# Cross attention of a two-layer decoder: all eight query projections ahead of the scores, in two PSUM banks in turn, with a new table of turns

## The chip, the cores and the metric

One core of one Trainium2 chip. The metric is the time on the device of one execution, in microseconds; less is better. The kernel before took 611.25 us, the median of three runs (607.7 to 611.59 us).

## The reference, cut to what matters

The decoder has two layers. Each is a self attention, a cross attention to a context, and a feed-forward part, with a layer norm ahead of each and the result added to x. The change touches the cross attention of the first layer (16 heads of 64, model width 128, four batches of 256 tokens, a context of 256 tokens, a mask that is False everywhere here):

```python
x = x + _L0_attn_ref(...)                          # stage l0a, relative position bias
q = layernorm(x) @ Wq                              # 128 -> 1024, 16 heads of 64
k = ctx @ Wk
v = ctx @ Wv
s = q @ k.T * 64**-0.5                             # per head, causal and padding mask
x = x + (softmax(s) @ v) @ Wo + bo                 # stage l0x
x = x + bit_linear / depthwise conv feed-forward   # stage ffn
...                                                # layer 1: stages l1a, l1x, moe
```

## The kernel before, in words

The four batches are split into two lanes, A and B, of two batches (512 tokens) each. Both lanes run the same six stages (l0a, l0x, ffn, l1a, l1x, moe) on the same core; each lane has its own four PSUM banks (`bank[0]` to `bank[3]`, printed as A_banks and B_banks) and its own part of SBUF. Lane A runs ahead of lane B by about one stage, so that a stage of A stands beside another stage of B.

For each engine each lane has a program that yields between its steps, and `merged` (line 2423) takes steps of the programs in the turns that the table `TURNS` (line 2389) gives for that engine: "A4 W1 A5" is four steps of lane A, one of the weight preparation, five of lane A. Each engine carries out its merged list strictly in that order: an instruction that waits for a semaphore holds up all that stand behind it. The numbers that the programs yield (`PAIRS`, `STEP`) order steps inside a lane, where two programs of it are interleaved (`interleaved`, line 113).

The stage l0x is `cross_attention` (line 718). Its TensorE program:

- `context` (line 940): 16 jobs, eight that project the values (L951) and eight that project the keys (L953), each one matmul of 128x512 in float32, in banks 0 to 2 in turn, copied out by ScalarE (L826).
- `queries(c)` (line 956), for c = 0 to 7: one matmul of 128x512 (L966), copied out by VectorE with the scale (L868). Query 0, 2 to 7 use bank 2, query 1 uses bank 3 (`q_bank`, line 781).
- `scores(p)` (line 976), for 16 pairs of heads p (8 for each of the lane's two batches): L984 and L986, in banks 0 and 1. VectorE adds the mask and takes the largest of each row (L914), ScalarE takes the exponential with the sums (L835), VectorE inverts the sums (L932), GpSimd multiplies (L818).
- `transposed(u)` (line 989), two for each pair: three transposes (L998) into bank 2, copied out by ScalarE (L852).
- `weighted_values(g)` (line 1001): probabilities times values (L1011) in bank 3, copied out by VectorE (L928) into `oT`, which has the place of `qT`.
- `output` (line 1015): eight products for each of two tiles of tokens (L1019), after pair 12 for the first batch and at the end for the second.

The loop over the pairs (`pairs`, line 1023) runs with a lag of two: in step p it issues the transposes of pair p - 2, the scores of pair p, query p + 2 (while there is one) and the weighted values of pair p - 3. So queries 0 and 1 stand ahead of the loop and queries 2 to 7 inside it. Bank 2 holds both the queries and the transposed weights; their users wait for one another:

```python
elif c < LAG + 2:
    pe.wait_ge(*s_qo(c))
else:
    pe.wait_ge(*s_pt(2 * (c - 1 - LAG)))     # queries: transposed weights copied out
...
if u % 2 == 0 and u // 2 + LAG + 1 < HP:
    pe.wait_ge(*s_qo(u // 2 + LAG + 2))      # transposes: query copied out
```

Other lines that the prediction names: L226 scores of stage l0a for the row maxima (one bank, one job after another), L330 the maxima on VectorE, L316 the second scores of l0a for the exponentials (L364 on ScalarE), L292 its weighted values, L712 the transposes of its output, L668 transposes of its queries and keys, L653 its projections; L1244 transposes in ffn of the convolved hidden layer; L231 the first scores of l1a.

## Time and profile before

| | us |
|---|---|
| median of three runs | 611.25 (607.7 to 611.59) |
| the profiled execution | 614.77 |
| its span, first to last instruction | 613.0 |
| TensorE busy in the span | 533.3 |
| VectorE busy | 420.4 |
| ScalarE busy | 328.5 |
| GpSimd busy | 193.8 |

The profiled execution took 614.77 us, 1.8 us more than its span, and 3.5 us more than the median of the runs. PE is TensorE's matmuls, PEld its loads of weights, DVE is VectorE, ACT ScalarE, POOL GpSimd. L966 is line 966 of the kernel. A float32 matmul appears as two records (x2). Times of records overlap where an engine is pipelined, so what an instruction costs a full engine is read from start to start. "[0.40 <-DVE ...]" behind a record is the idle time of its engine just ahead of it and what ended it. PEclk is the granted clock of TensorE as a share of full speed; the lower of its two levels is 0.5 (1.2 of 2.4 GHz).

### The profile page before, as it was taken

How to read it: one execution, taken by the hardware profiler on the slowest of the kernel's cores; microseconds unless marked ns; L12 is line 12 of the kernel's file. 1: busy time of each engine (PE TensorE's matmuls, PEld its weight loads, DVE VectorE, ACT ScalarE, POOL GpSimd, SP SyncE). 2: the span in 40 equal slices, each digit the busy share in tenths (PEclk: the TensorE clock that was granted, in tenths of full speed). 3: DMA queues.
4: the chain of work that ended last, by engine and by line, in shares of the span. 5: the costliest groups of instructions: out<-in, count | busy, mean ns of one | idle time of the engine just before them, and what ended most of it. 6: DMA issues, size and time to landing. Idle time of an engine off the chain costs nothing.

```text
span 613.0 us, 12971 instructions
## 1 busy us (share of the span) xinstructions
PE 533.3 (87%) x4858; PEld 328.1 (54%) x4858; DVE 420.4 (69%) x1229; ACT 328.5 (54%) x809; POOL 193.8 (32%) x288
## 2 busy tenths in 40 slices
PE   4767797998999989877995679988998989999995
PEld 2433344344555656556453556666666866755554
DVE  5784664574454774898769876757548677589796
ACT  2413444457767785597644346544675548364341
POOL 5553300042235454332621031001023221434765
PEclk9966889999999999889997799999999999999998
DMA  8700000000002000000237105210000000402101
GB/s 290 280 1 3 2 3 3 2 3 2 2 18 120 2 1 2 2 1 1 66 111 267 26 12 163 79 31 2 4 3 2 2 2 3 139 0 80 59 2 34
DMA packets 25816, 27.92 MB, mean 46 GB/s; under 512 B 18177, under 2 KB 22794, under 8 KB 24858
## 3 DMA queue, kind: packets, MB, share of 16 engines
q1 hardware_dynamic: 25754, 27.10, 13.3%
q8 instruction: 39, 0.64, 0.4%
q14 instruction: 23, 0.19, 0.1%
HBM read 22.14 MB, written 4.75 MB: 44 GB/s over the span
## 4 chain that ended last, share of the span: by engine, by line
PE 66%; DVE 17%; ACT 5%; issue 4%; DMA 2%; POOL 2%; SPq 2%; POOLq 0%; DVEq 0%; ACTq 0%
PE B_banks L2086 5%; PE A_banks L292 4%; PE A_banks L2086 4%; PE B_banks L292 3%; DVE A_l0a_nmax L330 3%; PE A_banks L1011 2%; PE A_banks L998 2%; PE B_banks L1852 1%; PE B_banks L2118 1%; PE B_banks L998 1%; PE A_banks L951 1%; PE A_banks L1852 1%; PE A_banks L953 1%; PE B_banks L953 1%; PE B_banks L1862 1%
## 5 line engine op out<-in xcount | busy, mean ns | idle before, releaser
L818 POOL TENSOR_TENSOR A_l0x_prob<-A_l0x_prob,A_l0x_inverted_sums 128x256 f32<-128x256 f32 (+1 forms) x32 | 25.9, 829 | 54.1 <-DVE A_l0x_inverted_sums L932 54.0
L818 POOL TENSOR_TENSOR B_l0x_prob<-B_l0x_prob,B_l0x_inverted_sums 128x256 f32<-128x256 f32 (+1 forms) x32 | 27.1, 866 | 41.1 <-DVE B_l0x_inverted_sums L932 41.1
L2086 PE MATMUL A_banks<-A_moe_xT,w_moe_rows 128*128 128x512 f32 x72 | 35.1, 600 | 0.0
L330 DVE TENSOR_REDUCE B_l0a_nmax<-B_banks 128x2 f32<-128x512 f32 x32 | 21.5, 688 | 19.3 <-PE B_banks L226 13.6
L2086 PE MATMUL B_banks<-B_moe_xT,w_moe_rows 128*128 128x512 f32 x72 | 34.5, 596 | 0.0
L364 ACT ACTIVATE A_l0a_expT<-A_banks 128x512 f32<-128x512 f32 x32 | 18.3, 598 | 26.9 <-PE A_banks L316 26.9
L835 ACT ACTIVATE B_l0x_prob<-B_l0x_prob,B_l0x_nmax 128x128 f32<-128x128 f32 x64 | 28.3, 444 | 6.2 <-DVE B_l0x_nmax L914 6.2
L330 DVE TENSOR_REDUCE A_l0a_nmax<-A_banks 128x2 f32<-128x512 f32 x32 | 21.4, 689 | 13.8 <-PE A_banks L226 12.0
L835 ACT ACTIVATE A_l0x_prob<-A_l0x_prob,A_l0x_nmax 128x128 f32<-128x128 f32 x64 | 28.2, 446 | 2.2 <-DVE A_l0x_nmax L914 2.2
L364 ACT ACTIVATE B_l0a_expT<-B_banks 128x512 f32<-128x512 f32 x32 | 18.6, 599 | 11.6 <-PE B_banks L316 11.5
L998 PE MATMUL B_banks<-w_const_rows,B_l0x_prob 128*128 128x128 f32 x96 | 17.4, 292 | 7.9 <-ACT B_l0x_probT L852 5.0
L914 DVE CUSTOM_DVE_ANT_0 A_l0x_prob<-A_banks,A_l0x_mask_q 128x128 f32<-128x128 f32 x64 | 19.0, 353 | 7.2 <-PE A_banks L986 6.0
L1982 ACT ACTIVATE B_moe_h<-B_banks,w_moe_rest_rows 128x512 f32<-128x512 f32 x18 | 12.3, 684 | 20.3 <-PE B_banks L2086 20.3
L1715 POOL TENSOR_TENSOR A_l1x_prob<-A_l1x_prob,A_l1x_rz 128x512 f32<-128x512 f32 x8 | 8.3, 1042 | 46.2 <-DVE A_l1x_rz L1796 46.2
L852 ACT ACTIVATE B_l0x_probT<-B_banks 128x384 f32<-128x384 f32 x32 | 15.5, 484 | 13.5 <-PE B_banks L998 13.5
L364 ACT ACTIVATE A_l1a_expT<-A_banks 128x384 f32<-128x384 f32 x32 | 14.9, 494 | 13.9 <-PE A_banks L272 13.9
L364 ACT ACTIVATE B_l1a_expT<-B_banks 128x384 f32<-128x384 f32 x32 | 15.3, 494 | 11.7 <-PE B_banks L272 11.5
L852 ACT ACTIVATE A_l0x_probT<-A_banks 128x384 f32<-128x384 f32 x32 | 15.6, 488 | 11.0 <-PE A_banks L998 11.0
L330 DVE TENSOR_REDUCE B_l1a_nmax<-B_banks 128x2 f32<-128x512 f32 (+1 forms) x24 | 16.1, 686 | 6.1 <-PE B_banks L234 6.0
L914 DVE CUSTOM_DVE_ANT_0 B_l0x_prob<-B_banks,B_l0x_mask_q 128x128 f32<-128x128 f32 x64 | 18.9, 349 | 1.1 <-PE B_banks L986 0.9
L998 PEld LDWEIGHTS B_banks<-w_const_rows,B_l0x_prob 128*128 128x128 f32 x96 | 10.9, 146 | 15.9 <-issue 8.8
L2086 PEld LDWEIGHTS A_banks<-A_moe_xT,w_moe_rows 128*128 128x128 f32 x72 | 12.7, 190 | 11.9 <-issue 10.8
(612 smaller groups left out, 1574.5 us busy)
## 6 DMA issues: line engine op xcount, KB each, us to landing
w_toeplitz_rows<-in_toeplitz_rows SPq DMA_DIRECT2D x1, 3072.0 KB, 15.7
w_moe_rows<-in_moe_rows SPq DMA_DIRECT2D x1, 2304.0 KB, 8.6
w_l1x_rows<-in_l1x_rows SPq DMA_DIRECT2D x1, 2048.0 KB, 8.6
A_l1x_values<-A_l1a_v_tokens SPq DMA_DIRECT2D x4, 512.0 KB, 2.6
A_l1x_v_groups<-A_l1x_values SPq DMA_DIRECT2D x16, 128.0 KB, 3.2
B_l1x_values<-B_l1a_v_tokens SPq DMA_DIRECT2D x4, 512.0 KB, 3.2
B_l1x_v_groups<-B_l1x_values SPq DMA_DIRECT2D x16, 128.0 KB, 3.2
w_l0x_vo_rows<-in_l0x_vo_rows SPq DMA_DIRECT2D x1, 1024.0 KB, 8.8
```

The source lines that it names most:

```text
L292: ins = pe.matmul(bank[r:r + self.rows, second:S], lhsT, rhs, start=(part == 0), stop=(part == parts - 1), skip_group_check=True)
L330: dve.tensor_reduce(out, scores, AX, ALU.max, negate=True).then_inc(self.s_mx.sem, 1)
L364: act.activation(self.expT[:, u % self.ring, :], self.exp_bank(u)[:, 0:self.W], ACT.Exp, scale=self.scale).then_inc(self.s_p.sem, 1)
L818: ins = pool.tensor_tensor(pair, pair, bcast(rz[:, g % 2, i, :], 2, n), ALU.mult)
L835: ins = act.activation(part, part, ACT.Exp, bias=nmax[:, b, i, h:h + 1], scale=-1.0, accum_out=zsum[:, g % 2, i, u % 2:u % 2 + 1])
L852: act.activation(probT[:, u % 4, :], bank[2][:, 0:W], ACT.Copy).then_inc(s_pt.sem, 1)
L914: ins = dve.tensor_tensor_reduce(prob[:, (2 * p + j) % RING, at:at + n], bank[j][:, at:at + n], mask_q[:, b, at:at + n], 1.0, 3e38, ALU.ad ...
L953: ins = pe.matmul(bank[n % 3][:, :], w["l0x_k"][:, c * P:(c + 1) * P], cT[:], start=True, stop=True)
L998: ins = pe.transpose(bank[2][:, c * P:(c + 1) * P], prob[:, u % RING, c * P:(c + 1) * P], w["ident"][:])
L1011: ins = pe.matmul(bank[3][HD * j:HD * (j + 1), part * P:S], vals[:, b * SB + part, h * HD:(h + 1) * HD], pT[:, S:W] if part else pT[:, 0:S ...
L1982: act.activation(h1[:, n % 2, :], hidden_bank(2 * n)[:, :], ACT.Identity, bias=w["moe_b1"][:, e, part:part + 1]).then_inc(s_h1.sem, 1)
L2086: pe.matmul(hidden_bank(k)[:, :], w["moe_w3" if which else "moe_w1"][:, ORDER[i], part, :], xT[:], start=True, stop=True).then_inc(s_h.sem, 1)
```

## The change

All eight queries are projected ahead of the first scores, in banks 2 and 3 in turn. Bank 2 then holds transposed weights only, and the waits between transposes and queries go, but for one: the first transpose waits until the last query is copied out. VectorE's copies of the queries stand ahead of its first maxima likewise. `PAIRS` goes from 10 to 17, so that the steps of the loop sort behind the queries in a lane. No instruction is added or dropped: each engine has the same instructions as before, in another order. The table of turns is new for tensor, vector, scalar and gpsimd, from the first stage to the last; sync's is unchanged.

```diff
-    PAIRS, STEP = 10.0, 4.5
+    PAIRS, STEP = 17.0, 4.5
 ...
     def q_bank(c):
-        return bank[3 if c == 1 else 2]
+        return bank[2 + c % 2]
 ...
     def vector(dve):
-        for c in range(2):
+        for c in range(HP):
             yield 7.8 + 1.0 * c
             queries(c)
 ...
-            if p + 2 < HP:
-                yield PAIRS + STEP * p + 2.4
-                queries(p + 2)
 ...
     def tensor(pe):
         def queries(c):
-
-            if c == 1:
-                pe.wait_ge(*s_xT(1))
-            elif c == 2:
-                pe.wait_ge(*s_qo(1))
-            elif c < LAG + 2:
-                pe.wait_ge(*s_qo(c))
-            else:
-                pe.wait_ge(*s_pt(2 * (c - 1 - LAG)))
+            if c >= 2:
+                pe.wait_ge(*s_qo(c - 1))
 ...
         def transposed(u):
             pe.wait_ge(*s_pn(u // 2 + 1))
-            if u % 2 == 0 and u // 2 + LAG + 1 < HP:
-                pe.wait_ge(*s_qo(u // 2 + LAG + 2))
-            elif u // 2 == HP - 1 - LAG and u % 2 == 0:
+            if u == 0:
+                pe.wait_ge(*s_qo(HP))
+            elif u == 2 * (HP - 1 - LAG):
                 pe.wait_ge(*s_m(1))
 ...
             pe.wait_ge(*s_kvo(JOBS - 1))
-            queries(0)
-            queries(1)
+            for c in range(HP):
+                yield 7.0 + 1.0 * c
+                queries(c)
 ...
-                if p + 2 < HP:
-                    yield PAIRS + STEP * p + 1.0
-                    queries(p + 2)
 ...
 TURNS = {
     "tensor":
-        "A4 W1 A5 W1 A23 B1 A3 B1 A3 B2 A4 B2 A3 B2 A1 B1 A6 B1 ...
+        "A4 W1 A5 W1 A23 B1 A3 B1 A1 B1 A2 B1 A1 B3 A1 B1 A1 B1 ...
```

Twelve lines fewer stand ahead of the later stages, so line 998 of before is line 988 after, 1011 is 1001, 1244 is 1232, 966 is 956.

How the order changes is shown at three places, all on TensorE.

First, in the stage l0a of both lanes, after lane A's shifts have been transposed (L244, L248). Before:

```order
L244 MATMUL A_banks<-w_ident_bf,A_l0a_parts 128x128 x2
L248 MATMUL A_banks<-w_other_token,w_ident_bf 128x512 x8
L316 MATMUL A_banks<-A_l0a_qkT 128x256 x4
L226 MATMUL A_banks<-A_l0a_qkT 128x256 x2
L668 MATMUL B_banks<-w_ident_bf,B_l0a_expT 128x128 x8
L226 MATMUL A_banks<-A_l0a_qkT 128x256 x2
L316 MATMUL A_banks<-A_l0a_qkT 128x256 x4
L226 MATMUL A_banks<-A_l0a_qkT 128x256 x2
L668 MATMUL B_banks<-w_ident_bf,B_l0a_expT 128x128 x8
L226 MATMUL A_banks<-A_l0a_qkT 128x256 x2
L653 MATMUL B_banks<-w_l0a_rows,B_l0a_xT 128x384
L226 MATMUL A_banks<-A_l0a_qkT 128x256 x2
```

After:

```order
L244 MATMUL A_banks<-w_ident_bf,A_l0a_parts 128x128 x2
L248 MATMUL A_banks<-w_other_token,w_ident_bf 128x512 x8
L668 MATMUL B_banks<-w_ident_bf,B_l0a_expT 128x128 x12
L316 MATMUL A_banks<-A_l0a_qkT 128x256 x4
L668 MATMUL B_banks<-w_ident_bf,B_l0a_expT 128x128 x4
L226 MATMUL A_banks<-A_l0a_qkT 128x256 x2
L653 MATMUL B_banks<-w_l0a_rows,B_l0a_xT 128x384
L226 MATMUL A_banks<-A_l0a_qkT 128x256 x2
L668 MATMUL B_banks<-w_ident_bf,B_l0a_expT 128x128 x8
L316 MATMUL A_banks<-A_l0a_qkT 128x256 x4
L226 MATMUL A_banks<-A_l0a_qkT 128x256 x2
L668 MATMUL B_banks<-w_ident_bf,B_l0a_expT 128x128 x8
```

Lane B's transposes of queries and keys (L668) and its projections (L653) move ahead of lane A's second scores: the projection stands behind lane A's first row of L226 after, and behind its fourth before. Over the whole stage lane B's part of l0a runs further ahead of lane A's than before.

Second, where lane A's first pairs meet the end of lane B's l0a. Before, from behind the first scores of lane A to its first transposes:

```order
L712 MATMUL B_banks<-w_const_rows,B_l0a_xT 128x128 x2
L966 MATMUL A_banks<-A_l0x_xT,w_l0x_rows 128x512
L316 MATMUL B_banks<-B_l0a_qkT 128x256 x4
L292 MATMUL B_banks<-B_l0a_expT,B_l0a_vals 32x256 x8
L292 MATMUL B_banks<-w_toeplitz_rows,B_l0a_vals 32x256 x8
L316 MATMUL B_banks<-B_l0a_qkT 128x256 x4
L984 MATMUL A_banks<-A_l0x_kT,A_l0x_qT 128x128 x2
L986 MATMUL A_banks<-A_l0x_kT,A_l0x_qT 128x256 x2
L966 MATMUL A_banks<-A_l0x_xT,w_l0x_rows 128x512
L712 MATMUL B_banks<-w_const_rows,B_l0a_xT 128x128 x2
L316 MATMUL B_banks<-B_l0a_qkT 128x256 x4
L998 MATMUL A_banks<-w_const_rows,A_l0x_prob 128x128 x3
```

After, from the first scores to the first transposes:

```order
L974 MATMUL A_banks<-A_l0x_kT,A_l0x_qT 128x128 x2
L976 MATMUL A_banks<-A_l0x_kT,A_l0x_qT 128x256 x2
L712 MATMUL B_banks<-w_const_rows,B_l0a_xT 128x128 x2
L316 MATMUL B_banks<-B_l0a_qkT 128x256 x4
L974 MATMUL A_banks<-A_l0x_kT,A_l0x_qT 128x128 x2
L976 MATMUL A_banks<-A_l0x_kT,A_l0x_qT 128x256 x2
L292 MATMUL B_banks<-B_l0a_expT,B_l0a_vals 32x256 x8
L292 MATMUL B_banks<-w_toeplitz_rows,B_l0a_vals 32x256 x8
L316 MATMUL B_banks<-B_l0a_qkT 128x256 x4
L712 MATMUL B_banks<-w_const_rows,B_l0a_xT 128x128 x2
L316 MATMUL B_banks<-B_l0a_qkT 128x256 x4
L988 MATMUL A_banks<-w_const_rows,A_l0x_prob 128x128 x3
```

Two projections of queries (L966) stood between the scores and these transposes; they are gone from there, all eight now stand ahead of the first scores, and the next scores of lane A follow sooner.

Third, where lane B's later pairs meet lane A's ffn, around B's first output (L1019 before, L1009 after) and A's transposes of the convolved layer (L1244 before, L1232 after). Before:

```order
L998 MATMUL B_banks<-w_const_rows,B_l0x_prob 128x128 x3
L1011 MATMUL B_banks<-B_l0x_probT,B_l0x_vals 64x256 x2
L1011 MATMUL B_banks<-B_l0x_probT,B_l0x_vals 64x128 x2
L1244 MATMUL A_banks<-w_const_rows,A_ffn_conv 128x128 x16
L998 MATMUL B_banks<-w_const_rows,B_l0x_prob 128x128 x3
L984 MATMUL B_banks<-B_l0x_kT,B_l0x_qT 128x128 x2
L986 MATMUL B_banks<-B_l0x_kT,B_l0x_qT 128x256 x2
L1019 MATMUL B_banks<-w_l0x_vo_rows,B_l0x_qT 128x128 x16
```

After:

```order
L1009 MATMUL B_banks<-w_l0x_vo_rows,B_l0x_qT 128x128 x16
L988 MATMUL B_banks<-w_const_rows,B_l0x_prob 128x128 x3
L1001 MATMUL B_banks<-B_l0x_probT,B_l0x_vals 64x256 x2
L1001 MATMUL B_banks<-B_l0x_probT,B_l0x_vals 64x128 x2
L988 MATMUL B_banks<-w_const_rows,B_l0x_prob 128x128 x3
L974 MATMUL B_banks<-B_l0x_kT,B_l0x_qT 128x128 x2
L976 MATMUL B_banks<-B_l0x_kT,B_l0x_qT 128x256 x2
L988 MATMUL B_banks<-w_const_rows,B_l0x_prob 128x128 x3
L1001 MATMUL B_banks<-B_l0x_probT,B_l0x_vals 64x256 x2
L1001 MATMUL B_banks<-B_l0x_probT,B_l0x_vals 64x128 x2
L1232 MATMUL A_banks<-w_const_rows,A_ffn_conv 128x128 x16
```

Before, A's transposes stand ahead of B's first output; after, they stand two steps of B's loop behind it. Up to lane A's first scores of l1a (L231) the list of TensorE's instructions then is the same again but for its order.

## Rows read from the trace of the kernel before

**Rows 1.** Page, part 1, busy time; part 2, the granted clock in 40 slices.
```profile
PE 533.3 (87%) x4858; PEld 328.1 (54%) x4858; DVE 420.4 (69%) x1229; ACT 328.5 (54%) x809; POOL 193.8 (32%) x288
...
PEclk9966889999999999889997799999999999999998
```
**Rows 2.** Windows: start:end, length, busy of each engine (instructions), PEclk, DMA share, GB/s.
```profile
0.00:44.00 44.00, 26.01 (x150) 15.76 (x151) 31.55 (x80) 12.60 (x32) 24.06 (x42) 0.88 0.54 199
44.00:110.00 66.00, 53.73 (x515) 25.34 (x514) 37.13 (x89) 28.98 (x69) 10.78 (x26) 0.82 0.01 2
110.00:245.00 135.00, 130.68 (x967) 69.95 (x967) 78.33 (x346) 92.41 (x287) 50.01 (x66) 1.00 0.05 17
245.00:355.00 110.00, 86.51 (x628) 57.99 (x627) 90.55 (x293) 62.56 (x173) 30.96 (x64) 0.89 0.21 66
355.00:613.00 258.00, 236.41 (x2606) 159.07 (x2604) 182.79 (x423) 131.90 (x250) 77.98 (x90) 0.99 0.12 37
51.00:64.00 13.00, 11.61 (x74) 5.04 (x74) 6.04 (x11) 3.75 (x11) 2.28 (x6) 0.50 0.00 1
75.00:81.00 6.00, 5.96 (x52) 2.72 (x54) 2.48 (x7) 1.08 (x2) 0.00 (x0) 0.50 0.02 4
```
**Rows 3.** Line 966, the queries: what TensorE idled for ahead of them (us, times).
```profile
  ACT A_l0x_probT L852: 0.8, 3
  ACT B_l0x_probT L852: 0.7, 2
```
**Rows 4.** Waits of TensorE between 40 and 60 us (us, times, longest).
```profile
PE A_banks L226 <- DVE A_l0a_nmax L330: 2.2, 5, 0.8
PE A_banks L316 <- DMA A_l0a_qkT<-A_l0a_shiftT: 1.8, 1, 1.8
```
**Rows 5.** Timeline of TensorE, 136 to 147 us.
```profile
136.39 0.39 PE L984 MATMUL A_banks<-A_l0x_kT,A_l0x_qT 64*128 64x128 f32 x4
...
141.91 1.07 PE L292 MATMUL B_banks<-B_l0a_expT,B_l0a_vals 128*32 128x256 f32 x16
...
143.78 0.39 PE L316 MATMUL B_banks<-B_l0a_qkT 64*128 64x256 bf16 x4
144.00 0.39 PE L984 MATMUL A_banks<-A_l0x_kT,A_l0x_qT 64*128 64x128 f32 x4
...
145.72 0.38 PE L712 MATMUL B_banks<-w_const_rows,B_l0a_xT 128*128 128x128 f32 x2
146.03 0.39 PE L316 MATMUL B_banks<-B_l0a_qkT 64*128 64x256 bf16 x4
146.82 0.52 PE L998 MATMUL A_banks<-w_const_rows,A_l0x_prob 128*128 128x128 f32 x3 [0.40 <-DVE A_l0x_qT L868]
```
**Rows 6.** Timeline of TensorE, 190 to 194 us.
```profile
190.15 0.87 PE L1011 MATMUL A_banks<-A_l0x_probT,A_l0x_vals 128*64 128x256 f32 x8
190.95 1.12 PE L953 MATMUL B_banks<-B_ctxT,w_l0x_rows 128*128 128x512 f32 x2
191.91 0.49 PE L998 MATMUL A_banks<-w_const_rows,A_l0x_prob 128*128 128x128 f32 x3
192.33 0.49 PE L984 MATMUL A_banks<-A_l0x_kT,A_l0x_qT 64*128 64x128 f32 x4
...
193.19 1.12 PE L953 MATMUL B_banks<-B_ctxT,w_l0x_rows 128*128 128x512 f32 x2
```
**Rows 7.** Timeline of all engines: one pair of lane B, from its scores to its transposes.
```profile
260.72 0.49 PE L984 MATMUL B_banks<-B_l0x_kT,B_l0x_qT 64*128 64x128 f32 x4
...
262.93 0.40 ACT L835 ACTIVATE B_l0x_prob<-B_l0x_prob,B_l0x_nmax 128x128 f32<-128x128 f32 x1 [0.27 <-DVE B_l0x_nmax L914]
...
264.70 0.47 ACT L852 ACTIVATE B_l0x_probT<-B_banks 128x384 f32<-128x384 f32 x1
...
265.36 0.17 DVE L932 RECIPROCAL B_l0x_inverted_sums<-B_l0x_zsum 128x4 f32<-128x4 f32 x1
...
267.27 0.55 PE L998 MATMUL B_banks<-w_const_rows,B_l0x_prob 128*128 128x128 f32 x3 [0.65 <-POOL B_l0x_prob L818]
```

More of the change, by code:

```diff
@@ L2390 @@
     "tensor":
[8 rows of a table removed]
-    "vector":
[9 rows of a table removed]
-    "scalar":
[5 rows of a table removed]
[8 rows of a table added]
+    "vector":
[9 rows of a table added]
+    "scalar":
[5 rows of a table added]
     "gpsimd":
-        "A15 B2 A1 B14 A11 B2 A2 B2 A1 B1 A2 B1 A1 B1 A1 B1 A2 B1 A1 B2 A2 B1 A1 B6 A1 B2 A1 B1 A3 B2 A2 B8 A8 B2 A2 B1 A1 B3 A2 B2 A1 B3 A2 B1 A1 B2 A6 B1 A2 "
-        "B2 A2 B2 A1 B2 A1 B6 A1 B2 A1 B2",
+        "A12 B2 A3 B1 A1 B13 A14 B2 A2 B3 A3 B1 A1 B1 A1 B3 A1 B2 A2 B9 A3 B2 A1 B1 A3 B7 A6 B2 A2 B1 A1 B2 A1 B1 A1 B2 A2 B1 A1 B2 A1 B1 A1 B2 A6 B1 A5 B6 A2 "
+        "B6 A1 B2 A1 B2",
     "sync":
```

44 rows, old and new, of the table TURNS are left out of this document.

## Prediction

> **What bounds the kernel now.** I read the busy time of the engines first, then windows by stage, then the waits of TensorE, then the timeline at the places that the change moves. The page shows TensorE busy for 533.3 of 613.0 us [rows 1]; its list of instructions stays the same. What an order can change is then its idle time, 613.0 - 533.3 = 79.7 us, and the time that it works at the lower clock. The windows say where these lie [rows 2]: 18.0 us idle from 0 to 44 (the loads), 12.3 from 44 to 110 (l0a of both lanes), 4.3 from 110 to 245 (A's l0x beside the end of B's l0a and the start of B's l0x), 23.5 from 245 to 355 (B's l0x beside A's ffn and l1a), 21.6 behind 355. The lower level of the clock was granted at 51 to 64 us and at 75 to 81 us, behind stretches in which TensorE waited for maxima and for a transfer [rows 4], and in parts of 245 to 355, whose mean is 0.89; from 110 to 245 it was 1.00 [rows 2].
>
> So the stage that the edit is about, the queries of lane A and most of lane B's, lies where TensorE is 97% busy (130.7 of 135 us). There is little to win there and something to lose; the parts with slack are the first 110 us and those behind 245, which the edit itself doesn't touch and the new turns do.
>
> **The change part by part.**
>
> *The waits between queries and transposes.* Bank 2 no longer changes hands between the two. Ahead of the queries TensorE idled 0.8 + 0.7 us for the copies of transposed weights [rows 3], and once 0.40 us ahead of a transpose for the copy of a query [rows 5]: 1.9 us in all. Bounds: -1.9 to 0. I take -1.0, since these waits lie in the loop over the pairs, where the next wait (for GpSimd's product) is near.
>
> The profile shows these gaps as short and few. The Trainium skill (Perfetto Trace Analysis, Optimization Strategy) says that a gap which repeats can mean that PSUM lacks room for the next tile; by that rule a bank of its own for the transposed weights would be worth the whole gap, here the 1.9 us. The same section advises to interleave stretches that are limited by different engines, and this speaks against the edit: it takes pure TensorE work out of a loop in which TensorE waits for the other engines. No row before shows the loop without it beside B's l0a.
>
> *The queries move ahead of the loop.* No projection is added or dropped. One takes 0.96 us of a full TensorE, as a key projection of the same form does from 190.95 to 191.91 [rows 6]. Twelve of them (2 to 7 of each lane) leave the loop, 11.5 us of work that filled the time between a pair's scores and its transposes. In the row ahead of the loop they cost the same 0.96 us each; VectorE's copy of 0.69 us each fits beside them in two banks. That time is neutral as long as what they leave behind doesn't idle.
>
> *What they leave behind, lane A.* The chain of a pair: scores, maxima, exponentials, sums, product, transposes. One pair of lane B took 267.27 - 260.72 = 6.55 us; 265.36 - 264.70 = 0.66 us of it VectorE was busy with the ffn of A, so 5.9 us is the near bound [rows 7]. A's first pair took 146.82 - 136.39 = 10.4 us, with other exponentials ahead of its own on ScalarE; that is the far bound [rows 5]. Now what stands between in the new order. Prices from start to start: scores 0.86 (192.33 to 193.19), transposes 0.42, weighted values 0.80 [rows 6]; both L292 1.87, L316 0.22, L712 0.31 [rows 5]. First scores to first transposes after: 0.86 + 0.31 + 0.22 + 0.86 + 1.87 + 0.22 + 0.31 + 0.22 = 4.9 us. Against 6.55 us TensorE idles 1.7. The same count for A's pair 2 gives 5.9 us (two scores, three transposes, one weighted values, L292 and L316), 0.7 idle; pair 4 gives 7.1, none. Sum +2.4 us. Bounds: 1.0 + 0 at 5.9 us, and 5.5 + 4.5 at 10.4 us: +1.0 to +10. I take +2.4, by the row of lane B, since fewer exponentials of l0a stand ahead of A's than before.
>
> *The same for lane B.* Its first pair has 5.5 us of TensorE work to its transposes: idle 1.1 us. Behind it both lanes are in their loops without queries: per pair TensorE has 0.86 + 2 x 0.42 + 0.80 = 2.5 us; ScalarE has the exponentials, 264.70 - 262.93 = 1.77 us, and two copies of 0.47 [rows 7], 2.7 us. ScalarE is then the fuller one by 0.2 us a pair, about 1 us over the five pairs of both lanes. +2 us; bounds 0 to +6 (4.9 idle at the chain of 10.4, and that 1 us).
>
> *The turns of l0a (44 to 110 us).* Lane B's projections and first scores move forward by some 7 us of TensorE's work, lane A's second half goes back by 3 to 4. More stands between one of A's maxima and the next, so that the waits for L330 and for the shift's transfer (2.2 and 1.8 us from 40 to 60 us [rows 4]) are filled: twelve of B's transposes now stand ahead of A's first L316. VectorE is busy 37.1 of these 66 us and can take it. Bounds: no gain beside 1 us lost, to all 12.3 us of idle time [rows 2]. I take -3.5, between a quarter and a third of the idle time: waits for maxima remain in one bank, one job after another.
>
> *The turns behind 245 us.* B's pairs stand closer, A's ffn further back: its transposes (L1244) now stand behind B's first output and about 9 us of TensorE's work later. At A's first scores of l1a the lists are level again, and VectorE is busy 90.6 of 110 us there [rows 2], so that what is filled at one end is missed at the other. I take 0, bounds -4 to +6. Behind 355 us A's l1x is later and B's earlier by 5 us or so, and A's experts end earlier; TensorE is 92% busy: 0, bounds -3 to +3.
>
> *Sum.* -1.0 + 2.4 + 2.0 - 3.5 + 0 + 0 = -0.1 us, against the profiled execution's own 614.8 us: 614.7. That execution lay 3.5 us above the median of the runs, so a median of 611.2; I say 611.0 us. A measurement of this kernel can tell about 1% (6.1 us) from no change.
>
> **The rivals.**
>
> *Faster: the front fills and the clock stays up.* TensorE worked 11.6 + 6.0 us at the lower level in the two windows at 0.50 [rows 2]; at full speed that work is done in half, 8.8 us less. If B's work closes the gaps ahead of these windows, the idle time taken as -3.5 comes with a good part of this, say -5, and the total is 603 us. For it: the drops at 51 and 75 us follow gaps of TensorE in just the stretch where B's work comes in. Against: A's chain of maxima in one bank stays, so TensorE still pauses. The Trainium skill (TensorE: Matmul & The Clock Gate, What's actually happening) says that activity lifts the clock, which the trace agrees with (1.00 through the fullest stretch, 110 to 245); by that rule a denser front gets its clock back as well, which would be the 603 us.
>
> *Slower: the pairs starve.* If a pair's chain with B's l0a on ScalarE stays near the 10.4 us of A's first pair instead of 6.55, the idle time of A's first pairs is 10 us and B's 5 to 6, where 4.4 were counted: 10 to 12 us more, 621 us. It decides from a chain of about 8.5 us on. For it: in the new order eight of A's pairs, not five, meet the end of B's l0a, so ScalarE has 8 x 2.7 us beside the l0a exponentials in some 33 us. Against: even so it has a few us to spare, and from 110 to 245 it was 68% busy.
>
> *A's ffn decides.* A's ffn ends about 8 us later, and B's earlier end doesn't pay for it, because A's l1a is the longer chain up to 355 us: +5, 616 us. Against: TensorE has less to do between the two.
>
> **How the numbers follow.** The forecast about 0.37, the late ffn 0.08 (of which half falls over 1%), starving pairs 0.21, the filled front 0.34. Within 1%: 0.37 + 0.04 = 0.41; slower by over 1%: 0.21 + 0.04 = 0.25; faster by over 1%: 0.34. The likeliest case by itself gives 605 to 617. The range takes in both outer cases, 601 to 621 us, with about a tenth left out at either side.
>
> **What would show it.** Right: TensorE busy 533 us again; at 44 to 110 us less idle time than 12 us; a few us of idle time of TensorE ahead of A's first transposes (L988 after), ended by GpSimd's product, where before there was none; no wait between queries and copies of transposed weights; idle time behind 245 us near 23. Wrong: idle time over 12 us in A's loop beside B's l0a (the slower rival); a granted clock near 1 from 44 to 110 us (the faster one); VectorE below 80% busy behind 245 us with A's l1a late (the third).

## The result: about 1% slower

The changed kernel took 615.07 us, the median of four runs (612.65 to 618.73), beside 610.01 us for the kernel before (607.7 to 611.59): a ratio of 1.0096, 95% interval 1.0068 to 1.0124, or +5.9 us. Measured again beside other runs of before (609.47 us) it took 616.11 us, a ratio of 1.0102 (1.0081 to 1.0123), +6.2 us. The forecast was no change (611.0 us, a sum of -0.1 us); 6 us more came, on the edge of what was called "within 1%", and both intervals exclude no change.

The first thing to see is that the two profiled executions don't show this. The page of the changed kernel, its busy time and its granted clock:

```profile
span 612.2 us, 12956 instructions
PE 529.8 (87%) x4844; PEld 324.9 (53%) x4858; DVE 420.7 (69%) x1229; ACT 326.0 (53%) x807; POOL 192.7 (31%) x288
...
PEclk9978899999999999997997789999999999999998
```

Its span is 0.8 us *shorter* than the one of before [rows 1]. (Its busy time can't be held against 533.3 us as it stands: 14 of 4858 matmul records are missing.) The profiled execution of before (614.77 us) was 5 us above the median of before, that of after (613.99 us) was 1 us below its own. Windows of the changed kernel over the same stretches as [rows 2]:

```profile
...
44.00:110.00 66.00, 54.45 (x563) 25.80 (x562) 39.83 (x98) 30.69 (x71) 8.83 (x22) 0.90 0.01 3
110.00:245.00 135.00, 126.47 (x926) 68.97 (x924) 77.10 (x349) 88.99 (x282) 49.85 (x66) 1.00 0.05 17
245.00:355.00 110.00, 87.96 (x656) 57.33 (x658) 92.28 (x297) 64.99 (x176) 30.93 (x66) 0.91 0.21 66
355.00:612.20 257.20, 233.48 (x2551) 155.99 (x2557) 181.19 (x407) 127.47 (x243) 77.99 (x90) 0.99 0.11 37
```

From 44 to 110 us the clock was 0.90 where it had been 0.82, and TensorE did 563 instructions where it had done 515. From 110 to 245 us it idled 8.5 us where it had idled 4.3. So more idle time stands where TensorE had been full, in the place that the slower rival named.

Stretches between fixed clock times hold different work, though. For the reading that follows each trace is cut at the same three instructions: lane A's last key projection (L953 before, L950 after), lane A's first scores of l1a (L231), and lane B's last product of ffn (L1260, L1248). From one to the next every kernel here carries out the same number of TensorE's instructions, within two by the records (nine records of after's tail are missing). The stretches front (from the first L653), middle (queries and both cross attentions) and tail, before and then after, TensorE alone (start:end, length, busy, granted clock, DMA):

```profile
10.25:133.75 123.50, 101.27 (x791) 0.86 0.14 55
133.75:331.17 197.42, 176.77 (x1349) 0.98 0.12 41
356.34:612.99 256.65, 235.07 (x2586) 0.99 0.12 37
```

```profile
10.17:127.24 117.07, 96.90 (x790) 0.90 0.15 57
127.24:328.00 200.76, 177.54 (x1347) 0.98 0.10 32
351.43:612.19 260.76, 236.35 (x2577) 0.99 0.11 36
```

The front is 6.4 us shorter, the middle 3.3 longer, the tail 4.1 longer. The stretch from lane A's first scores of l1a to lane B's last product of ffn is in none of the three; it was 25.2 us before and 23.4 after. Which of these differences belong to the order and which to one execution's clock, one trace of each kernel can't say. That is what the experiments are for.

What ended TensorE's waits in the middle, before (130 to 245 us) and after (126 to 250 us), us, times, longest:

```profile
PE B_banks L712 <- ACT B_l0a_xT L555: 1.4, 2, 1.0
PE B_banks L998 <- ACT B_l0x_probT L852: 1.4, 1, 1.4
PE A_banks L998 <- DVE A_l0x_qT L868: 0.4, 1, 0.4
PE A_banks L998 <- ACT A_l0x_probT L852: 0.3, 1, 0.3
PE B_banks L966 <- ACT B_l0x_probT L852: 0.3, 1, 0.3
```

```profile
PE A_banks L988 <- ACT A_l0x_probT L852: 3.3, 5, 2.0
PE B_banks L988 <- ACT B_l0x_probT L852: 1.9, 3, 0.7
PE B_banks L988 <- POOL B_l0x_prob L818: 1.2, 1, 1.2
PE B_banks L712 <- ACT B_l0a_xT L555: 1.0, 1, 1.0
PE A_banks L974 <- DVE A_l0x_nmax L914: 0.8, 1, 0.8
```

The waits between queries and transposes are gone (0.4 + 0.3 us), and 5.2 us of waits for ScalarE's copies of transposed weights stand ahead of the transposes, where there had been 1.7: they find the one bank still full. (That is the edit and the new turns together; e5 below separates them.) The longest of them, seen at all engines around 225 us of the changed kernel:

```profile
223.08 0.49 ACT L852 ACTIVATE A_l0x_probT<-A_banks 128x384 f32<-128x384 f32 x1 [0.87 <-PE A_banks L988]
223.47 0.39 ACT L835 ACTIVATE B_l0x_prob<-B_l0x_prob,B_l0x_nmax 128x128 f32<-128x128 f32 x1
...
224.34 0.47 ACT L852 ACTIVATE B_l0x_probT<-B_banks 128x384 f32<-128x384 f32 x1
...
224.71 0.39 ACT L835 ACTIVATE A_l0x_prob<-A_l0x_prob,A_l0x_nmax 128x128 f32<-128x128 f32 x1
...
226.46 0.47 ACT L852 ACTIVATE B_l0x_probT<-B_banks 128x384 f32<-128x384 f32 x1
...
226.84 0.48 ACT L852 ACTIVATE A_l0x_probT<-A_banks 128x384 f32<-128x384 f32 x1
...
227.46 0.52 PE L988 MATMUL A_banks<-w_const_rows,A_l0x_prob 128*128 128x128 f32 x3 [1.98 <-ACT A_l0x_probT L852]
```

ScalarE works almost without a pause (4.32 of the 4.4 us from 223.0 to 227.4), in the order of its list: B's exponentials, B's copy, A's exponentials, B's copy, and only then A's copy for which TensorE waits. TensorE has nothing between. Over a longer stretch ScalarE isn't full: 16.1 of the 22 us from 210 to 232 us, where it was busy 17.4 us before. The gap takes the new turns as well as the edit: with the edit and the old turns (e5) the longest such wait of lane A is 0.7 us.

### The profile page after: what moved, and what is told of

Its sections match the earlier page's. It is cut to its first block, busy times and chain, and to the rows that moved or that the text cites. A ratio compares the mean times of both kernels' runs of the same rounds, so it can differ in the third digit from the quotient of the medians.

```text
span 612.2 us, 12956 instructions
## 1 busy us (share of the span) xinstructions
PE 529.8 (87%) x4844; PEld 324.9 (53%) x4858; DVE 420.7 (69%) x1229; ACT 326.0 (53%) x807; POOL 192.7 (31%) x288
## 4 chain that ended last, share of the span: by engine, by line
PE 61%; DVE 20%; ACT 7%; issue 6%; DMA 2%; POOL 2%; SPq 2%; POOLq 0%; DVEq 0%; ACTq 0%
PE A_banks L2074 5%; PE A_banks L292 4%; PE B_banks L292 3%; PE B_banks L2074 3%; DVE A_l0a_nmax L330 3%; PE A_banks L988 2%; ACT B_l0x_prob L835 2%; PE A_banks L1001 1%; DVE B_l1a_nmax L330 1%; PE B_banks L956 1%; PE A_banks L1799 1%; PE A_banks L956 1%; PE A_banks L1850 1%; PE B_banks L1009 1%; PE A_banks L1009 1%
## 5 line engine op out<-in xcount | busy, mean ns | idle before, releaser
L330 DVE TENSOR_REDUCE A_l0a_nmax<-A_banks 128x2 f32<-128x512 f32 x32 | 21.3, 686 | 8.8 <-PE A_banks L226 7.0
L1970 ACT ACTIVATE A_moe_h<-A_banks,w_moe_rest_rows 128x512 f32<-128x512 f32 x18 | 12.3, 682 | 18.7 <-PE A_banks L2074 18.7
L330 DVE TENSOR_REDUCE A_l1a_nmax<-A_banks 128x2 f32<-128x512 f32 (+1 forms) x24 | 16.2, 686 | 6.7 <-PE A_banks L234 6.6
```

The lines of the kernel that those rows point to most:

```text
L330: dve.tensor_reduce(out, scores, AX, ALU.max, negate=True).then_inc(self.s_mx.sem, 1)
L1970: act.activation(h1[:, n % 2, :], hidden_bank(2 * n)[:, :], ACT.Identity, bias=w["moe_b1"][:, e, part:part + 1]).then_inc(s_h1.sem, 1)
```

## The experiments

All kernels but two differ from before or after in the table of turns alone. A splice carries one table up to a point and the other behind it; steps that the first table had not yet issued follow in the second one's order. "Front" is up to lane A's first query (some 134 us), "middle" up to 341 or 345 us, "tail" behind. At both seams the lists of before and after stand at nearly the same step in both lanes. All ran in five rounds beside before; the ratio's interval stands behind each time. Where a cost is given in us, it is the ratio times 609.7 us.

**Three parts and the whole.** The tensor table at the place of the first seam, e1 (the other engines likewise); e2 has the old line instead of the new one in the changed kernel, and both e2 and e3 change tables at 341 to 345 us:

```diff
-        "A4 W1 A5 W1 A23 B1 A3 B1 A3 B2 A4 B2 A3 B2 A1 B1 A6 B1 A4 B1 A1 B1 A4 B1 A1 B1 A1 B1 A5 B2 A5 B2 A1
+        "A4 W1 A5 W1 A23 B1 A3 B1 A1 B1 A2 B1 A1 B3 A1 B1 A1 B1 A2 B2 A2 B2 A1 B1 A3 B1 A1 B1 A1 B1 A2 B1 A2
...
```

e3, tensor, against before, where the tail begins:

```diff
-        "B3 A2 B1 A1 B1 A17 B2 A4 B1 A17 B1 A4 B4 A2 B1 A6 B1 A1 B1 A2 B3 A3 B2 A2 B2 A2 B3 A2 B3 A5 B1 A2 B4
+        "B3 A2 B1 A1 B1 A17 B2 A4 B1 A17 B1 A4 B4 A2 B1 A3 B1 A4 B4 A2 B1 A1 B1 A4 B1 A2 B1 A2 B2 A1 B1 A1 B3
...
```

> The code of before, with the new turns only up to lane A's first query (some 134 us), the old ones behind. In the profiles the new order stands 6.1 to 6.5 us ahead at 130 us in both lanes, of which about 5 us can be the clock of that one execution (the lower level for 34 us up to 110 us before, for 23 us after). Theory one (the front is filled, and the loss lies behind it): 6 us faster, 604 us beside before at 610. Theory two (the gain is the clock of one execution, or is lost again because the old order behind it doesn't use it): within 1.5 us of before.

> The new code of cross attention with the new turns from lane A's first query to lane A's first scores of l1a (134 to 341 us), the old turns ahead of it and behind. Theory one (the pairs without queries starve beside lane B's l0a: both lanes lost 10 us from 134 to 170 us and won 7 back from 170 to 245): 3 to 7 us slower than before, 613 to 617. Theory two (the loss of the whole change lies in the tail): within 1.5 us of before.

> The code and the turns of before up to 345 us, the new turns behind (from lane A's first shift of l1a to the end). In the profiles the new order lost 4 us there, from 4.8 ahead at 350 us to 0.7 ahead at the end. Theory one (the late l1x of lane A costs that): 4 us slower than before, 614. Theory two (the two lanes' ends level out): within 1.5 us of before.

> The changed kernel once more, beside the same runs of before as the three parts. All theories: 4 to 6 us slower than before (615 beside 610). The sum of what the three parts cost by themselves should be that; if it isn't, the parts depend on one another.

| | median, us | ratio (95%) | us |
|---|---|---|---|
| before | 609.47 | | |
| e1, front | 607.23 | 0.995 (0.9931 to 0.9969) | -3.0 |
| e2, middle | 618.43 | 1.0143 (1.0112 to 1.0175) | +8.7 |
| e3, tail | 613.52 | 1.0069 (1.0048 to 1.0089) | +4.2 |
| e4, after again | 616.11 | 1.0102 (1.0081 to 1.0123) | +6.2 |

The front wins 3.0 us (1.9 to 4.2), half of theory one and twice the bound of theory two. The middle lost more than either theory said, the tail what theory one said. The parts sum to +9.9 where the whole is +6.2. The windows between the fixed instructions show how much of each is order. Front and middle of e1 (new front, old middle), then of e3 (old front and middle), and the middle of e2:

```profile
13.62:128.44 114.82, 94.06 (x792) 0.90 0.12 45
128.44:323.82 195.38, 174.05 (x1348) 1.00 0.13 41
350.15:606.79 256.64, 235.07 (x2586) 0.99 0.11 37
```

```profile
13.36:130.11 116.75, 94.11 (x792) 0.90 0.12 45
130.11:325.27 195.16, 173.88 (x1348) 1.00 0.13 41
350.71:611.24 260.53, 237.09 (x2586) 0.99 0.12 36
```

```profile
129.58:333.00 203.42, 178.25 (x1349) 0.98 0.10 31
```

e3 has the front of before, in the same order: it took 116.75 us and not 123.50, at a clock of 0.90 and not 0.86. (Its first L653 also came 3.1 us later; at the end of the front e3 stood 3.6 us ahead of before, 130.11 for 133.75.) Of the 6.4 us by which the front seemed to win in the two first traces, the rows of e3 and e1 at equal clock leave 1.9 to the order (116.75 - 114.82), and that is idle time (22.6 and 20.8 us). Over all traces the front ended at 129.6 to 135.1 us in the old order (twelve traces) and at 125.3 to 128.4 us in the new (six).

The middle in the old order is 195.2 to 195.4 us at full clock, and 203.4 in the new: 3.9 us more idle time (25.2 for 21.3) and 4.4 us more busy time for the same instructions, at a clock of 0.98. The busy part can't all be laid to the order, since the old order isn't always granted the full clock there: before itself had 0.98 and 176.8 us of busy time. And some 2 us come back behind the middle: the stretch from lane A's first scores of l1a to lane B's last product of ffn took 26.3 and 25.4 us in e1 and e3, and 23.5 in e2. The tail is 256.6 us in the old order, as it was in before, and 260.5 in the new.

**The middle taken apart.** The new code with all other steps in the old turns (e5: the table of the changed kernel is replaced by the old one, the queries drawn ahead); the old code with the new turns of the middle (e6); and the new middle in two halves, up to 241 us (e7, against e2) and behind 245 us (e8, against before). Their tensor tables where they part (here and below the long lines are cut at the right):

e5 against the changed kernel:

```diff
-        "A4 W1 A5 W1 A23 B1 A3 B1 A1 B1 A2 B1 A1 B3 A1 B1 A1 B1 A2 B2 A2 B2 A1 B1 A3 B1 A1 B1 A1 B1 A2 B1 A2
+        "A4 W1 A5 W1 A23 B1 A3 B1 A3 B2 A4 B2 A3 B2 A1 B1 A6 B1 A4 B1 A1 B1 A4 B1 A1 B1 A1 B1 A5 B2 A5 B2 A1
...
```

e7 against e2:

```diff
-        "A2 B1 A1 B3 A1 B3 A1 B1 A1 B1 A2 B4 A4 B1 A2 B2 A3 B1 A3 B2 A1 B1 A1 B2 A3 B3 A1 B2 A1 B15 A1 B2 A1
+        "A2 B1 A1 B3 A1 B3 A1 B1 A1 B1 A2 B4 A4 B1 A2 B2 A3 B1 A3 B2 A1 B1 A1 B2 A3 B3 A1 B2 A1 B13 A2 B3 A1
...
```

e8 against before (e6 has the old lines up to the first query, then the new ones, so far as the lane's steps allow):

```diff
-        "A2 B1 A1 B2 A2 B1 A1 B1 A2 B1 A2 B1 A3 B2 A2 B1 A1 B2 A2 B4 A3 B1 A3 B1 A2 B1 A1 B11 A2 B3 A1 B11 A1
+        "A2 B1 A1 B2 A2 B1 A1 B1 A2 B1 A2 B1 A3 B2 A2 B1 A1 B2 A2 B4 A3 B1 A3 B1 A2 B1 A1 B13 A1 B2 A1 B3 A1
...
```

> The new code of cross attention with all other steps in the old turns (the six queries of a lane drawn together ahead of its first scores, nothing else moved). Theory one (the edit itself costs: TensorE has nothing for the gap between a pair's scores and its transposes): 5 to 9 us slower than before, 615 to 619. Theory two (the new turns of the middle cost): within 2 us of before.

> The old code (queries in the loop, old banks and waits) with the new turns from 134 to 341 us and the old ones elsewhere. Theory one (the edit itself costs): within 2 us of before. Theory two (the turns cost): 5 to 9 us slower, as the middle as a whole was (8.7).

> New code, new turns only up to the end of lane A's cross attention (some 241 us), then the old ones. Theory one (the pairs starve in the first half; TensorE idled 1.8 us more from 134 to 175 us and 1 more from 175 to 245): 5 to 9 us slower than before. Theory two (the loss is made behind 245 us, where lane A's transposes of the ffn stand behind lane B's first output: they began 15 us later in the middle's trace, A's first scores of l1a 6 to 8): 1 to 3 us slower.

> Old code, old turns up to 245 us, new ones up to 341 us, old ones behind. Theory one (the loss lies ahead of 245 us): within 2 us of before. Theory two (it lies behind): 4 to 8 us slower.

| | median, us | ratio (95%) | us |
|---|---|---|---|
| e5, the edit alone | 614.95 | 1.008 (1.0058 to 1.0103) | +4.9 |
| e6, old code, new turns of the middle | 627.42 | 1.0268 (1.0227 to 1.0308) | +16.3 |
| e7, first half of the middle | 616.83 | 1.0113 (1.007 to 1.0155) | +6.9 |
| e8, second half of the middle | 611.51 | 1.0026 (1.0 to 1.0053) | +1.6 |

The edit costs 4.9 us by itself (3.5 to 6.3), with the old turns: the lower end of theory one of e5. e6 refutes what both theories took for granted, that the new turns can be had without the edit: they count on six steps fewer in each lane's loop, and with the queries still there they cost 16.3 us. e7 and e8 sum to 8.5 us, the middle's 8.7. So the new turns of the middle do not repair the edit, they add to it: 3.8 us in all (e2 less e5, whose intervals stand apart). How that splits is less sure: 2.0 us up to 241 us (e7 less e5, whose intervals overlap) and 1.6 behind, which is within theory one of e8 and whose interval touches zero.

The middle of e5 and e7 between the same instructions, and what TensorE waited for in e5 from 130 to 246 us:

```profile
129.70:330.27 200.57, 176.16 (x1348) 0.99 0.12 40
```

```profile
131.84:334.41 202.57, 176.03 (x1348) 0.99 0.12 40
```

```profile
PE B_banks L712 <- ACT B_l0a_xT L555: 1.9, 4, 1.0
PE B_banks L988 <- ACT B_l0x_probT L852: 1.4, 1, 1.4
PE A_banks L988 <- ACT A_l0x_probT L852: 1.4, 4, 0.7
PE B_banks L292 <- DVE B_l0a_xn L618: 0.8, 2, 0.5
PE A_banks L974 <- DVE A_l0x_nmax L914: 0.7, 1, 0.7
PE A_banks L1001 <- DVE A_l0x_qT L925: 0.6, 1, 0.6
```

e5 is 5.3 us longer than the old middle at full clock (200.6 for 195.3): 3.1 us of idle time (24.4 for 21.3) and 2.2 us of busy time. The idle time goes with the edit: seven traces of the old middle have 20.7 to 21.3 us. It isn't one gap. The waits of this list sum to 6.8 us, those of before to 3.8; ScalarE's copies of transposed weights have 2.8 of them (1.7 before), and the rest of the growth is a few tenths each at lane B's L712 and L292, lane A's scores and its weighted values. No wait for GpSimd's product is in the list, where theory one looked for it. That a projection of 0.96 us had covered these waits is how I read the two lists; no run puts other work in its place.

The busy time can't be laid to the edit. The lower level was granted once in e5's middle, at 255 us, and before's own trace, with the old code and turns, has it at the same place (before, then e5):

```profile
252.00:262.00 10.00, 8.34 (x58) 0.83 0.01 2
```

```profile
252.00:262.00 10.00, 8.33 (x56) 0.83 0.01 2
```

**The edit for one lane at a time** (old turns). The code of both kernels stands side by side, chosen by lane; e10 has "B":

```diff
-    PAIRS, STEP = 10.0, 4.5
+    AHEAD = lane.name == "A"
+    PAIRS, STEP = 17.0 if AHEAD else 10.0, 4.5
...
-            if p + 2 < HP:
+            if p + 2 < HP and not AHEAD:
...
-            queries(0)
-            queries(1)
+            for c in range(HP if AHEAD else 2):
+                if AHEAD:
+                    yield 7.0 + 1.0 * c
+                queries(c)
```

> The new code for lane A alone, lane B's queries stay in its loop, all steps in the old turns. In the trace of the edit alone lane A's part beside lane B's l0a had cost some 2 us by the time lane B projected its last key, lane B's part 3 to 4 more. Theory one (each lane pays where its own first pairs stand): 1 to 3 us slower than before. Rival (lane A pays most, since lane B's l0a fills ScalarE there): 4 us or more.

> The new code for lane B alone, old turns. Theory one: 3 to 4 us slower than before; with the run for lane A it sums to the 4.9 us of the edit for both. Rival (a clock that falls behind the gaps of both together): both lanes' runs near before, the sum well under 4.9.

e9 took 609.89 us beside 609.76, a ratio of 1.0016 (0.9991 to 1.0042), +1.0 us; e10 612.15 us, 1.0032 (1.0012 to 1.0053), +2.0 us. Lane A's interval (-0.5 to +2.6 us) holds both no change and most of theory one, lane B is below its 3 to 4 us; the sum of 2.9 is short of the 4.9 for both, but by no more than the three intervals allow. The rival of e9 (4 us or more beside B's l0a) falls. The middle of e10, then that of e9, whose profiled execution was its slowest (616.36 us):

```profile
131.24:328.42 197.18, 173.94 (x1349) 1.00 0.13 40
```

```profile
135.08:332.86 197.78, 176.03 (x1348) 0.99 0.12 40
```

The busy time of e10 is that of the old order at full clock, with 1.9 us more idle time (23.2 for 21.3). e9 has 0.5 us more idle time and 2.1 us more busy time: there the lower level was granted at 257 us, as in before and e5, with lane A alone changed. So the rival of e10, a clock that falls only with the gaps of both lanes, finds no support; whether the edit costs more for both lanes than the sum for each stays open.

**The tail in two halves**, new turns from 345 to some 470 us (e11), and behind 470 us (e12), tensor against before.

e11:

```diff
-        "B3 A2 B1 A1 B1 A17 B2 A4 B1 A17 B1 A4 B4 A2 B1 A6 B1 A1 B1 A2 B3 A3 B2 A2 B2 A2 B3 A2 B3 A5 B1 A2 B4
+        "B3 A2 B1 A1 B1 A17 B2 A4 B1 A17 B1 A4 B4 A2 B1 A3 B1 A4 B4 A2 B1 A1 B1 A4 B1 A2 B1 A2 B2 A1 B1 A1 B3
...
```

e12:

```diff
-        "B1 A1 B8 A2 B1 A2 B1 A1 B2 A1 B1 A1 B4 A1 B1 A3 B1 A1 B1 A1 B3 A3 B4 A2 B1 A2 B1 A1 B1 A7 B1 A2 B1 A
+        "B1 A1 B10 A1 B3 A1 B1 A2 B1 A1 B3 A1 B1 A1 B3 A1 B1 A3 B2 A3 B3 A1 B1 A3 B1 A8 B1 A1 B5 A8 B1 A2 B1
...
```

> Old code and turns, with the new turns from 345 to some 470 us only (l1a and the start of l1x). Theory one (the tail's 4.2 us is made where lane A's l1x is pushed back by 12 us for lane B's l1a): 3 to 5 us slower. Rival (it is made in the experts): within 1.5 us.

> Old code and turns up to 470 us, the new turns behind (end of l1x and the experts, where lane A's end 16 us earlier). Theory one: within 1.5 us of before. Rival: 3 to 5 us slower.

e11 took 615.64 us, 1.0104 (1.0074 to 1.0134), +6.3; e12 617.32 us, 1.0133 (1.0104 to 1.0162), +8.1. Both theories fall: each half costs more than the two together (4.2). At 470 us the two orders stand at different steps (lane A's l1x is some 12 us later in the new one), and a seam there makes a bunch of one lane's steps that neither table has. The experiment says nothing of the tail's cause, only that a table can't be cut there. What the whole tail shows is in e3: TensorE's waits from 350 to 606 us in e3 that e1 (old tail) hasn't, both around the meeting of the two l1x,

```profile
PE B_banks L172 <- DVE B_l1x_prob L164: 1.0, 1, 1.0
PE B_banks L1837 <- POOL B_l1x_prob L1715: 0.9, 1, 0.9
PE A_banks L1837 <- POOL A_l1x_prob L1715: 0.7, 1, 0.7
```

With smaller differences either way e3's tail has 1.9 us more idle time (23.4 for 21.6) and 2.0 us more busy time. The idle time repeats: 23.4 to 23.5 us in the four traces of the new tail that have all records (e3, e4, e14, e15), 21.4 to 21.7 in eleven of the old one. The busy time doesn't: 235.7 to 237.1 us new and 234.2 to 236.1 old, each way with the granted clock. Which step of the table brings the waits was not tried.

**The other corners.** Front and middle new (e13: the changed kernel with the old tail), front and tail new (e14), middle and tail new (e15: the changed kernel with the old front), and e1's kernel again (e16). Tensor, e13 against the changed kernel; e14 has e1's and e3's changes, e15 is e2 with the new tail:

```diff
-        "B4 A1 B1 A14 B1 A1 B1 A1 B1 A35 B1 A1 B4 A2 B1 A3 B1 A4 B4 A2 B1 A1 B1 A4 B1 A2 B1 A2 B2 A1 B1 A1 B3
+        "B4 A1 B1 A14 B1 A1 B1 A1 B1 A35 B1 A1 B4 A2 B1 A6 B1 A1 B1 A2 B3 A3 B2 A2 B2 A2 B3 A2 B3 A5 B1 A2 B4
...
```

> The changed kernel with the old turns behind 341 us: new front, new middle, old tail. Theory one (the three parts add up): -2.7 + 8.9 = 6 us slower than before, 615.5, and the tail's 4.2 us would then have to come on top in the whole change, which measured 6.2 only. Theory two (the middle as measured by itself carries 3 to 4 us that come from its seam with the old front): 2 to 3 us slower, 612, and the tail's 4.2 us makes the whole 6.2.

> Old code, new turns up to 134 us and behind 345 us, the old middle. Theory one (parts add): -2.7 + 4.2 = 1.5 us slower. Theory two (seam effects): 0 to 1 us either side of that.

> The changed kernel with the old turns up to lane A's first query: new middle and tail. Theory one (parts add): 8.9 + 4.2 = 13 us slower. Theory two (the middle's 8.9 us holds the seam behind it, with the old tail): 9 us slower or less.

> The new turns up to 134 us alone, once more, as the version that may beat both kernels: 2 to 3 us faster than before.

| | median, us | ratio (95%) | us |
|---|---|---|---|
| e13, front and middle | 613.31 | 1.0058 (1.0037 to 1.0078) | +3.5 |
| e14, front and tail | 610.62 | 1.0006 (0.9988 to 1.0024) | +0.4 |
| e15, middle and tail | 620.09 | 1.0169 (1.0148 to 1.0189) | +10.3 |
| e16, front again | 605.42 | 0.9927 (0.9911 to 0.9943) | -4.5 |

With all eight corners each part can be read at four places, by taking differences. The front: -3.7 (mean of e1 and e16), -5.2 (e13 less e2), -3.8 (e14 less e3), -4.1 (e4 less e15), mean -4.2. The middle: +8.7, +7.2, +6.1, +5.8, mean +7.0. The tail: +4.2, +4.1, +1.6, +2.7, mean +3.1. The sum is +5.9, beside +5.9 and +6.2 measured. No theory was met in its numbers: e13 and e15 lie between adding up (6 and 13 us) and the smaller sums that theory two gave (2 to 3, and 9), so middle and tail do look dearer when each is measured alone, by 1 to 3 us. e14 is near the sum. e1 and e16, the new turns of the front with the old kernel behind, are faster than both kernels, and than before by 3.0 and 4.5 us.

## Why the prediction was wrong

By its own steps:

- **The turns of l0a: -3.5 forecast, -4.2 measured** (-3.0 to -5.2). The size came out; the reason holds in part. The first gaps of [rows 4] shrank from 2.2 + 1.8 us to 1.2 + 0.6, but waits at lane B's transposes (L668) came in, 1.0 us. Over the whole front 1.9 us of idle time went (e1 beside e3). The rest of the gain is busy time at the granted clock, which the term didn't have, so that the match in size is partly luck.

```profile
PE A_banks L226 <- DVE A_l0a_nmax L330: 1.2, 2, 0.8
...
PE B_banks L668 <- DVE B_l0a_qkT L465: 0.7, 2, 0.4
PE A_banks L316 <- DMA A_l0a_qkT<-A_l0a_shiftT: 0.6, 1, 0.6
```

- **The edit by itself: -1.0 + 2.4 + 2.0 = +3.4 forecast, +4.9 measured** (3.5 to 6.3), with lane A at +1.0 and lane B at +2.0 when alone. That TensorE would idle where the projections had stood was right; where and for what was mostly wrong. I looked for idle time ahead of each lane's *first* transposes, ended by GpSimd's product. In the changed kernel lane B has it (1.2 us, forecast 1.1); with the edit alone (e5) it is in neither lane. Lane A's first transposes after (145.40 us) began without a wait, because 1.8 us of other waits had come between (0.82 for maxima, 0.96 for lane B's xT). What grew instead were many small waits, most of all for ScalarE's copies out of the one bank of the transposes: 1.7 us before, 2.8 with the edit alone, 5.2 with the new turns as well.
- **The waits taken away: -1.0, of 1.9 us.** The term was over-read. The 0.8 + 0.7 us of [rows 3] are of both queues, loads of weights and matmuls, and 1.3 us of them stand ahead of loads. In the table of waits of the matmuls alone, 0.3 us stood ahead of L966, and 0.4 ahead of the transposes: 0.7 us was all there was to win.
- **The clock was not in the term at all**, and the runs don't price it. I priced the edit as idle time at full clock. In e5 2.2 of its 5.3 us, and in e2 4.4 of 8.2, are more busy time for the same instructions. But the old middle had 2.9 us of the same in before's own trace (176.8 for 173.9). With all the new turns of the middle the clock there was 0.96 to 0.98 (after, e2, e4, e13, e15), beside 0.98 to 1.00 in seven traces of the old order: a part of their cost is likely the clock's, for the edit alone nothing shows it. The rival with the clock in it was given to the faster side only.
- **The new turns of the middle: 0 forecast, +3.8 measured (e2 less e5)**, about +2.0 up to 241 us and +1.6 behind. For the first half I had no term: I took the new table to be neutral where it wasn't priced. For the second the mechanism was a named rival (A's ffn late), at +5 us. In e8 lane A's transposes of ffn (L1244) began 146.7 us behind its last key projection, in e3 136.8 us; the delay is what the rival said, and of its price about a third came (1.6 us, interval 0 to 3.2).
- **Behind 355 us: 0 forecast, bounds -3 to +3, +3.1 measured** (+4.2 by itself). This step failed outright. I took lane A's l1x later, lane B's earlier and a TensorE that was 92% busy to come to nothing, without one wait in the rows that said so. The new tail has 1.9 us more idle time in every trace; which of its steps brings it stays open.

So one sum of small terms was off by 6 us in all: 1.5 at the edit, 3.6 at the turns of the middle, 3.1 behind, less 0.7 at the front, and less 1.5 because the pieces of the middle sum to 8.5 us by themselves and the middle costs 7.0 on the mean of the corners. Two of six terms stood at exactly 0, and the turns of the first half had no term at all. All three turned out on the slow side. The chance for slower (0.25) was too low for a change that takes cover away from the fullest engine.

Of the rivals, the slower one named the right side and stretch, by a chain that wasn't there: it needed about 8.5 us from lane A's first scores to its first transposes, and the changed kernel took 7.3 (138.08 to 145.40) with other waits in it. Its 10 to 12 us didn't come; that the middle as a whole cost +7.0 is the sum of smaller waits and the new turns. The faster one rested on the profiled clock of before (0.50 at 51 to 64 and 75 to 81 us, 8.8 us of loss), and much of that was not the order's: e3 ran the same front with the clock at 0.90 instead of 0.86 and was 3.6 us ahead at its end. Its sum was wrong as well: 5 us off the forecast of 611.0 is 606, not 603.

The Trainium skill (Perfetto Trace Analysis, Optimization Strategy) had been weighed in two parts. Its rule that repeated gaps ask for more room in PSUM points at the right resource and at the wrong gap here: the bank freed for the transposed weights gained 0.7 us at most, and the waits for copies out of it grew from 1.7 us to 2.8 (e5). Its advice to interleave stretches that are limited by different engines is what the edit undid in the loop, and e5's +4.9 us is what that was worth.

What was foreseen in "what would show it": less idle time from 44 to 110 us than 12 (11.6, which shows little), no wait between queries and copies of transposed weights (the list of waits shows none), idle time behind 245 us near 23 (22.0 up to 355 us). What should have been read as "wrong" was there too: idle time in the loop beside B's l0a, though not 12 us of it.

## What to carry to other kernels

A matmul that waits for nothing, placed inside a loop of dependent steps, isn't only work; it is the cover for the copies and reductions of the others. Before moving it out, list for each gap it covered the engine that will be late next, and price the gaps a few tenths each over all the rounds, not only at the first one. When a change also brings a new table of order, a term of 0 for "levelled out" is not a price: either find the rows or widen the range to the side on which cover is lost. And cut two traces at the same instructions before comparing, and look at a second execution before crediting a stretch's clock to its order.

## What the runs showed of the hardware

The granted clock of one stretch differed between executions of the same instructions in the same order: the front of before ran at 0.86 in one execution and at 0.90 in another (101.3 and 94.1 us of busy time, rows above). Where the same clock was granted, the same order repeated closely: the middle in the old order took 195.38 us in e1 and 195.40 in e16, both at 1.00, the old tail 256.65, 256.64 and 256.62 in before, e1 and e16, all at 0.99. Where it wasn't, the time moved with it: the same middle took 196.12 us in e14 at 0.99 and 197.42 in before at 0.98, the old tail 255.80 in e7 at 1.00 and 257.50 in e5 at 0.98. The middle of e14:

```profile
127.26:323.38 196.12, 175.42 (x1348) 0.99 0.12 41
```

The lower level was often granted at a gap or just behind it. In all eighteen traces it was at the gap of 2.0 to 3.1 us ahead of lane A's first scores of l1a, or up to 2.5 us behind its end; in before that gap ends at 331.1 us:

```profile
328.00:345.00 17.00, 11.25 (x73) 0.60 0.47 153
```

Around 225 to 235 us it came with the new turns only. Six executions have the 1.98 us gap shown above; in five of them (e2, e4, e7, e13, e15) the lower level was granted 1 to 3 us behind its start, in the first one of after it wasn't. e6, with the new turns and the old code, had it behind a gap of 1.5 us. In the eleven with the old turns there, whose longest gap in this place is 1.4 us, it wasn't granted. That the gap brings the lower level isn't shown: gap and order come together. The stretch from 222 to 238 us in e4 and in the first execution of after, which is the same kernel:

```profile
222.00:238.00 16.00, 13.24 (x94) 0.79 0.01 2
```

```profile
222.00:238.00 16.00, 13.24 (x116) 1.00 0.01 2
```

In e4 TensorE was busy as long as in after, with 94 instructions done for 116. The middle of e4 took 206.1 us, 4 us of it more idle time than the old order at full clock and 6.8 us more busy time.

```profile
126.43:332.56 206.13, 180.80 (x1348) 0.96 0.10 31
```

The Trainium skill (TensorE: Matmul & The Clock Gate, What's actually happening) ties the clock to TensorE's activity, and these rows agree in direction; that the same order is granted different clocks in the middle of a kernel is what the runs add.
